# Fourth layer's dense attention: one head at a time instead of two by turns

## The chip, the cores and the metric

The kernel runs on one core of one Trainium2 chip. The metric is the device time of one execution in microseconds; a kernel's time is the median of its runs. Beside the times there is one profiled execution of the kernel, taken by the hardware profiler. All stretches below are microseconds from the start of that execution's span.

## What is computed

The program chains convolution-like and attention layers on a batch of 4 with 128 channels and 32x32 positions, that is 4 x 1024 tokens of 128 features. The change touches one of them, `_L3_attn_ref`, whose dense part is this:

```python
def global_mha(x, in_w, in_b, out_w, out_b, nh):      # B, S, D = 4, 1024, 128; nh = 8
    hd = D // nh                                       # 16
    q, k, v = qkv_proj(x, in_w, in_b)                  # each [B, S, nh, hd]
    scores = jnp.einsum('bqhd,bkhd->bhqk', q, k) / np.sqrt(hd)
    attn = jax.nn.softmax(scores, axis=-1)
    o = jnp.einsum('bhqk,bkhd->bqhd', attn, v).reshape(B, S, D)
    return o @ out_w.T + out_b
# beside it a local attention (window 5, 4 heads) on the same x; both are fused by a
# two-layer MLP with silu, added to x and normalised; a second MLP with silu follows
```

4 batches of 8 heads make 32 heads; each has a 1024 x 1024 matrix of scores. All of this is in float32; the kernel carries q and k as three bfloat16 parts stacked on 96 rows.

## The kernel before

The change lies in `fourth_layer_stream`, which writes out the order of every engine's work for the whole fourth layer. A **step** is one tile of 128 keys (`m`, 0 to 7) of one head: 256 steps in all, 64 in each batch. For a step TensorE multiplies two halves of 512 queries into the three banks of `f_ST` (`scores_transposed`, line 2179), ScalarE takes the exponential of each half into `f_probs` (line 2369), which holds four steps, and TensorE then multiplies `f_v_ext` (values of the head, 16 columns and a column of ones, padded to 32) by these probabilities and adds them up over the eight tiles in the bank `f_O` (`mix`, line 2196). `mix` is called for two steps at a time (`VISIT` = 2), on every odd step from the third on: a *visit*, of four float32 products, each of which is two records of the trace, so eight records. Where in `f_O` a product lands is set by

```python
h, m = steps[s]
for n in range(NC2):
    at = 32 * (NC2 * (h % SHARE) + n)
    last = nc.tensor.matmul(O[at:at + 32, :], f.v_ext[...], f.probs[...], start=(m == 0),
                            stop=(m == NT - 1), tile_position=(0, at))
```

so head parity and query half choose one of the four strips of 32 columns of the array and 32 partitions of the bank. In the order before, steps go through two heads of a group (`SHARE` = 2) by turns: tile 0 of the even head, tile 0 of the odd head, tile 1 of the even head, and so on; 16 steps (`IN_GROUP`) make a group.

The exponential needs a shift for each query, the maximum of its row. Therefore TensorE also computes the scores the other way round, queries on partitions (`scores`, line 2152), two halves for each tile of 128 queries, into the two banks of `f_ring`, and VectorE reduces each half (`maximum`, line 2486). After a head's last half VectorE splits the shifts into three bfloat16 parts (`parts`, lines 2495 to 2499), TensorE turns them into rows (`shift_rows`, line 2164, in the same `f_ring`), and ScalarE copies these to three more rows of `f_stacks` (`rows`, line 2346, two copies). `scores_transposed` of tile 0 of a head waits for that copy (`rows_off`). The list `items`, made by `schedule` and `schedule_rows`, sets which halves of maxima and which rows go with which step; `AHEAD` = 2 is the number of tiles by which the maxima run ahead of a whole group of 16 tiles. Before the first step, with no other stream work beside it, the list "first" holds the maxima and rows of two heads.

Beside the steps run the programs `pre` (normalisation, q, k, v of the next batch), `local` (local attention) and `tail` (output projection, MLPs, normalisations of the batch before). `Beside.turn` lets them go on after each half of a step; their due times are counted in halves of steps. After the last step, `tally` follows and the next layer begins. SP loads `f_stacks` for a group eight steps after the group four before it ended (`LOAD_AFTER`), and ScalarE carries `f_O` off two steps after each group (`carry_off`).

The first layer has an attention of the same make (`dense_attention`), with heads of 32 features: there the values are padded to 64 columns, one head is taken at a time, and a visit (line 702, `att_O`) is four products too, at columns 0, 64, 0, 64.

Of the kernel before, what the change touches and what calls it, by code (L numbers as in the profile page):

```python
# [14 lines left out]
B, IMG = 4, 32  # L15
N = IMG * IMG
NT = N // P
# [1775 lines left out]
class Fourth:  # L1793


    HD, HEADS, SHARE, GROUPS = 16, 8, 2, 4
    IN_GROUP = SHARE * NT
# [64 lines left out]
def fourth_layer(nc, k):  # L1862

    with ExitStack() as c:
        f = Fourth(nc, k, c)
        with ExitStack() as c2:
            fourth_layer_stream(nc, k, f, c2)
        clear(nc, f.semaphores)
        nc.all_engine_barrier(sem_only=True)


def fourth_layer_stream(nc, k, f, c):

    HD, HEADS, SHARE, GROUPS, IN_GROUP = f.HD, f.HEADS, f.SHARE, f.GROUPS, f.IN_GROUP
    STEPS, VISIT, PROBS, RING, HALVES, TURNS = f.STEPS, f.VISIT, f.PROBS, f.RING, f.HALVES, f.TURNS
    steps = [(b * HEADS + g * SHARE + j, m) for b in range(B) for g in range(GROUPS) for m in range(NT)
             for j in range(SHARE)]
    all_groups = B * GROUPS
    lag = VISIT + 1

# [2 lines left out]
    def schedule(step, lo, hi):  # L1883
        new = [("s", h, t, n) for h, t in (divmod(r, NT) for r in range(lo, min(hi, B * HEADS * NT)))
               for n in range(NC2)]
        at_step[step] = list(range(len(items), len(items) + len(new)))
        items.extend(new)

    def schedule_rows(step, h):
        rows_at[step] = rows_at.get(step, []) + [h]  # L1890
        item_of_rows[h] = len(items)
        items.append(("r", h))

    schedule("first", 0, IN_GROUP)
    for h in range(SHARE):
        schedule_rows("first", h)
    for s in range(len(steps)):
        r = s + IN_GROUP + f.AHEAD
        schedule(s, IN_GROUP if s == 0 else r, r + 1)
        if (s + 1) % NT == 0 and s + IN_GROUP < len(steps):  # L1900
            schedule_rows(s, (s + IN_GROUP) // NT)
    order, count = {}, {"s": 0, "r": 0}
    for i, item in enumerate(items):
        order[i] = count[item[0]]
# [1768 lines left out]
```

## Time and profile before

| | us |
|---|---|
| median of the runs | 2507.49 |
| the profiled execution, its own time | 2505.68 |
| its span, first to last instruction | 2503.9 |
| fourth layer, the two heads of maxima ahead of the first step | 1334 to 1361 |
| fourth layer, the 256 steps | 1362 to 2080 |
| tally, then the next layer | 2080 to 2504 |

The profile names instructions by line and tile: `f_O<-f_probs,f_v_ext 128*32 128x512` is a product with a 128x32 stationary and a 128x512 moving operand. Busy time is the union of an engine's records; a matmul's record includes its way through the array, so consecutive matmuls overlap, and the distance from one start to the next is what one costs in a stream. PEclk is the granted clock of TensorE, where 1.00 is 2.4 GHz and 0.50 is 1.2 GHz.

### The profile page before, as it was taken

What the parts mean: (1) busy time and instruction counts of PE and PEld (TensorE: products, weight loads), DVE (VectorE), ACT (ScalarE), POOL (GpSimd) and SP (SyncE); (2) the same over time, 40 slices, a digit from 0 to 9 for tenths busy, and PEclk for the clock granted to TensorE, in tenths of its full rate; (3) what the DMA queues carried; (4) which work ended last, traced back from release to release, by engine and by line L of the source; (5) the groups of instructions that cost most, each with busy time, mean ns of one, the idle gap of its engine ahead of it and who ended that gap; (6) DMA issues with size and microseconds to landing.
All of it is one profiled execution on the core that took longest, in us unless ns stands there. A gap on an engine that the chain in (4) does not pass through costs nothing. (4 is left out here: it accounts for less than half of the span.)

```text
span 2503.9 us, 26613 instructions
## 1 busy us (share of the span) xinstructions
PE 1892.9 (76%) x8906; PEld 869.7 (35%) x8906; DVE 1573.4 (63%) x3594; ACT 1021.7 (41%) x1662; POOL 714.1 (29%) x693
## 2 busy tenths in 40 slices
PE   1595786689578657579975888878878888978596
PEld 1121321332132124456641222322322325854356
DVE  3477778777776866645745575665566555634567
ACT  0241233314123314535542667656656662124251
POOL 2300630260063023014442312322322331137720
PEclk7696887789688878879975999989988987769797
DMA  3300300210030000021002111101011000024100
GB/s 100 92 3 25 83 9 20 60 40 2 25 92 1 20 8 1 1 81 39 1 17 75 41 30 38 32 27 39 28 28 37 4 4 14 2 62 52 10 4 35
DMA packets 55407, 80.26 MB, mean 32 GB/s; under 512 B 17201, under 2 KB 28455, under 8 KB 55024
## 3 DMA queue, kind: packets, MB, share of 16 engines
q1 hardware_dynamic: 44758, 69.14, 9.3%
q10 hardware_dynamic: 6426, 7.99, 1.4%
q0 software_dynamic: 4096, 1.58, 1.3%
q8 instruction: 62, 1.02, 0.2%
q14 instruction: 65, 0.53, 0.1%
HBM read 50.13 MB, written 24.68 MB: 30 GB/s over the span
## 5 line engine op out<-in xcount | busy, mean ns | idle before, releaser
L2486 DVE TENSOR_REDUCE f_half_max<-f_ring 128x1 f32<-128x512 f32 x512 | 334.8, 684 | 273.0 <-PE f_ring L2152 270.9
L2369 ACT ACTIVATE f_probs<-f_ST 128x512 f32<-128x512 f32 x512 | 292.8, 597 | 210.8 <-PE f_ST L2179 206.7
L2152 PE MATMUL f_ring<-f_stacks 96*128 96x512 bf16 x512 | 212.1, 415 | 54.5 <-DVE f_half_max L2486 28.1
L772 DVE TENSOR_REDUCE att_half_max<-att_ring 128x1 f32<-128x512 f32 x256 | 161.2, 683 | 101.5 <-PE att_ring L659 96.6
L2179 PE MATMUL f_ST<-f_stacks 99*128 99x512 bf16 x512 | 204.0, 403 | 10.4 <-ACT f_probs L2369 10.3
L755 ACT ACTIVATE att_probs<-att_ST 128x1024 f32<-128x1024 f32 x128 | 129.3, 1023 | 156.1 <-PE att_ST L684 155.9
L2196 PE MATMUL f_O<-f_probs,f_v_ext 128*32 128x512 f32 x1024 | 153.3, 674 | 0.1
L3202 POOL DMA_INDIRECT ti_row<-features,slot_from x128 | 126.9, 992 | 57.4 <-issue 57.4
L2152 PEld LDWEIGHTS f_ring<-f_stacks 96*128 96x128 bf16 x512 | 50.4, 99 | 258.8 <-DVE f_half_max L2486 162.6
L659 PE MATMUL att_ring<-stacks 96*128 96x512 bf16 x256 | 103.7, 471 | 46.5 <-DMA stacks<-parts_dram 25.9
L684 PE MATMUL att_ST<-stacks 96*128 96x512 bf16 (+1 forms) x512 | 137.8, 398 | 0.0
L702 PE MATMUL att_O<-att_probs,v_ext 128*64 128x512 f32 x512 | 132.7, 644 | 6.6 <-DVE att_den L791 6.6
L1242 DVE TENSOR_TENSOR loc_weighed<-loc_wide,l_pad 128x512 f32<-128x512 f32 x200 | 124.4, 683 | 14.6 <-PE loc_wide L1196 9.5
L1739 ACT ACTIVATE bm_h<-bm_ps,bn 128x512 f32<-128x512 f32 x128 | 99.5, 777 | 78.2 <-PE bm_ps L1706 72.9
L1762 POOL TENSOR_TENSOR bm_h<-bm_h,bm_mix 128x512 f32<-128x512 f32 x64 | 81.9, 1302 | 159.7 <-ACT bm_h L1739 159.7
L1053 POOL MEMSET loc_padded<- 104x1296 f32 x4 | 4.7, 1177 | 387.5 <-POOLq L43 387.5
L1224 POOL TENSOR_TENSOR loc_partial<-loc_partial,loc_weighed 128x512 f32<-128x512 f32 x88 | 110.0, 1271 | 10.1 <-DVE loc_weighed L1242 6.6
L1202 PE MATMUL loc_acc<-loc_weighed,turned 128*128 128x512 f32 x208 | 107.1, 599 | 0.4
L2757 PE MATMUL gm_ps<-xn_cm,x 128*128 128x512 f32 x128 | 66.0, 644 | 45.8 <-ACT turned L2805 35.4
L2060 PE MATMUL f_ring<-f_hot 128*64 128x64 bf16 x1024 | 90.5, 366 | 7.9 <-DVE f_hot L2504 7.9
L2060 PEld LDWEIGHTS f_ring<-f_hot 128*64 128x64 bf16 x1024 | 87.1, 272 | 22.4 <-issue 12.7
L2504 DVE TENSOR_SCALAR f_hot<-f_xn 128x256 bf16<-128x256 bf16 x512 | 72.3, 220 | 28.7 <-issue 14.7
(585 smaller groups left out, 3552.7 us busy)
## 6 DMA issues: line engine op xcount, KB each, us to landing
f_stacks<-f_parts SPq DMA_DIRECT2D x192, 64.0 KB, 2.2
parts_dram<-l_parts SPq DMA_DIRECT2D x8, 768.0 KB, 3.6
stacks<-parts_dram SPq DMA_DIRECT2D x24, 256.0 KB, 9.5
stacks<-parts_dram ACTq DMA_DIRECT2D x24, 256.0 KB, 10.5
f_parts<-f_parts SPq DMA_DIRECT2D x8, 768.0 KB, 3.4
es_raw<-L_ffn_edge_index SPq DMA_DIRECT2D x8, 512.0 KB, 4.2
bm_mix<-mix SPq DMA_DIRECT2D x8, 512.0 KB, 9.0
xn_cm<-x SPq DMA_DIRECT2D x1, 2048.0 KB
```

The lines of the kernel that those rows point to most:

```text
L684: last = nc.tensor.matmul(ST[:, s % 2, n * BANK:(n + 1) * BANK], k.stacks[0:rows, 1, per * h + j, m * P:(m + 1) * P], k.stacks[0:rows, 0, ...
L702: last = nc.tensor.matmul(O[at:at + width, :], k.v_ext[:, m, h, :], probs[:, s % probs_ring, n * BANK:(n + 1) * BANK], start=(m == 0), sto ...
L755: nc.scalar.activation(probs[:, s % probs_ring, :], ST[:, s % 2, :], ACT.Exp).then_inc(probs_ready, 1)
L772: nc.vector.tensor_reduce(half_max[:, h % 2, t, n:n + 1], ring[:, i % RING], AX.X, ALU.max, negate=True).then_inc(reduced, 1)
L1242: nc.vector.tensor_tensor(o_, a, v, ALU.mult).then_inc(weighed_ready, 1)
L2060: last = nc.tensor.matmul(bank[64 * a:64 * a + 64, 0:64], low, high, start=(start and m == ms[0]), stop=(stop and m == ms[-1]), tile_posit ...
L2152: nc.tensor.matmul(ring[:, i % RING], f.stacks[0:STACK, 0, at, t * P:(t + 1) * P], f.stacks[0:STACK, 1, at, n * BANK:(n + 1) * BANK], star ...
L2179: nc.tensor.matmul(ST[:, i % HALVES], f.stacks[0:STACK + 3, 1, h % HEADS, m * P:(m + 1) * P], f.stacks[0:STACK + 3, 0, h % HEADS, n * BANK ...
L2196: last = nc.tensor.matmul(O[at:at + 32, :], f.v_ext[:, h // HEADS % 2, m, h % HEADS, :], f.probs[:, s % PROBS, n * BANK:(n + 1) * BANK], s ...
L2369: nc.scalar.activation(f.probs[:, s % PROBS, n * BANK:(n + 1) * BANK], ST[:, i % HALVES], ACT.Exp).then_inc(probs_ready, 1)
L2486: nc.vector.tensor_reduce(f.half_max[:, h % 2, t, n:n + 1], ring[:, i % RING], AX.X, ALU.max, negate=True).then_inc(reduced, 1)
L3202: self.nc.gpsimd.indirect_dma_start(self.row[:, j, :], None, self.k.features, bass.IndirectOffsetOnAxis(ap=self.k.slot_from[:, j:j + 1], a ...
```

## The change

The steps go through the heads one after the other, all eight tiles of a head, then the next head. The maxima run ahead by one head and two tiles (8 + 2) instead of two heads and two tiles (16 + 2), and "first" holds one head. The rows of head h come with the step just before its first, 8h - 1; before, they came nine steps ahead of an even head and two ahead of an odd one. Sizes of buffers, `VISIT`, `AHEAD`, the groups, their loads and the programs beside the steps stay.

```diff
-    steps = [(b * HEADS + g * SHARE + j, m) for b in range(B) for g in range(GROUPS) for m in range(NT)
-             for j in range(SHARE)]
+    steps = [(h, m) for h in range(B * HEADS) for m in range(NT)]
@@
-    schedule("first", 0, IN_GROUP)
-    for h in range(SHARE):
-        schedule_rows("first", h)
+    schedule("first", 0, NT)
+    schedule_rows("first", 0)
     for s in range(len(steps)):
-        r = s + IN_GROUP + f.AHEAD
-        schedule(s, IN_GROUP if s == 0 else r, r + 1)
-        if (s + 1) % NT == 0 and s + IN_GROUP < len(steps):
-            schedule_rows(s, (s + IN_GROUP) // NT)
+        r = s + NT + f.AHEAD
+        schedule(s, NT if s == 0 else r, r + 1)
+        if (s + 1) % NT == 0 and s + NT < len(steps):
+            schedule_rows(s, (s + NT) // NT)
```

## Rows read from the trace of the kernel before

**Rows 1.** The page's first part: busy time, share of the span, instructions.

```profile
PE 1892.9 (76%) x8906; PEld 869.7 (35%) x8906; DVE 1573.4 (63%) x3594; ACT 1021.7 (41%) x1662; POOL 714.1 (29%) x693
```

**Rows 2.** Busy time by stretch: stretch, length, engines, PEclk, DMA share, GB/s.

```profile
1334.00:1362.00 28.00, 22.00 (x52) 4.29 (x52) 23.43 (x44) 2.31 (x4) 2.54 (x3) 0.50 0.29 82
...
1362.00:2080.00 718.00, 601.93 (x2969) 191.57 (x2968) 430.20 (x1013) 454.09 (x849) 197.29 (x243) 0.93 0.09 27
2030.00:2080.00 50.00, 40.11 (x182) 10.38 (x180) 18.56 (x84) 30.86 (x63) 24.73 (x38) 0.80 0.03 6
```

**Rows 3.** Lines, 1362 to 2080: busy us, mean ns | idle before, releaser.

```profile
L2486 DVE TENSOR_REDUCE f_half_max<-f_ring 128x1 f32<-128x512 f32 x479 | 313.5, 684 | 251.1 <-PE f_ring L2152 250.4
L2369 ACT ACTIVATE f_probs<-f_ST 128x512 f32<-128x512 f32 x512 | 292.8, 597 | 210.8 <-PE f_ST L2179 206.7
L2179 PE MATMUL f_ST<-f_stacks 99*128 99x512 bf16 x512 | 204.0, 403 | 10.4 <-ACT f_probs L2369 10.3
L2152 PE MATMUL f_ring<-f_stacks 96*128 96x512 bf16 x477 | 191.3, 401 | 31.2 <-DVE f_half_max L2486 24.3
L2196 PE MATMUL f_O<-f_probs,f_v_ext 128*32 128x512 f32 x1024 | 153.3, 674 | 0.1
```

**Rows 4.** TensorE's timeline between two visits: start, length, instruction, [idle before, releaser].

```profile
1450.22 1.06 PE L2196 MATMUL f_O<-f_probs,f_v_ext 128*32 128x512 f32 x8
1451.21 0.39 PE L2152 MATMUL f_ring<-f_stacks 96*128 96x512 bf16 x1
...
1452.39 0.39 PE L2152 MATMUL f_ring<-f_stacks 96*128 96x512 bf16 x1
1452.62 0.38 PE L2179 MATMUL f_ST<-f_stacks 99*128 99x512 bf16 x1
1453.70 0.39 PE L2152 MATMUL f_ring<-f_stacks 96*128 96x512 bf16 x1 [0.70 <-DVE f_half_max L2486]
...
1454.24 1.07 PE L2196 MATMUL f_O<-f_probs,f_v_ext 128*32 128x512 f32 x8
```

**Rows 5.** First layer's attention: the page's group of its visits, and TensorE's timeline.

```profile
L702 PE MATMUL att_O<-att_probs,v_ext 128*64 128x512 f32 x512 | 132.7, 644 | 6.6 <-DVE att_den L791 6.6
...
173.52 1.94 PE L702 MATMUL att_O<-att_probs,v_ext 128*64 128x512 f32 x8
175.39 1.92 PE L684 MATMUL att_ST<-stacks 96*128 96x512 bf16 x8
```

**Rows 6.** TensorE's timeline around a fall of its clock.

```profile
1480.53 0.60 PE L2164 MATMUL f_ring<-ident_b,f_shift_parts 128*3 128x128 bf16 x8 [0.90 <-DVE f_half_max L2486]
...
1481.60 1.94 PE L2196 MATMUL f_O<-f_probs,f_v_ext 128*32 128x512 f32 x8
1483.47 0.58 PE L2047 MATMUL f_side<-f_att_t,spread 60*128 60x512 bf16 x1
```

**Rows 7.** TensorE's timeline ahead of the first step.

```profile
1334.24 1.03 PE L2152 MATMUL f_ring<-f_stacks 96*128 96x512 bf16 x2 [18.76 <-DMA f_stacks<-f_parts]
...
1357.46 0.60 PE L2164 MATMUL f_ring<-ident_b,f_shift_parts 128*3 128x128 bf16 x8 [0.28 <-DVE f_half_max L2486]
1359.01 0.60 PE L2164 MATMUL f_ring<-ident_b,f_shift_parts 128*3 128x128 bf16 x8 [0.94 <-DVE f_shift_parts L2499]
```

**Rows 8.** Rows of a head: TensorE, ScalarE, and who waited for the copies.

```profile
1444.15 0.40 PE L2164 MATMUL f_ring<-ident_b,f_shift_parts 128*3 128x128 bf16 x8 [0.30 <-DVE f_half_max L2486]
...
1444.80 1.07 PE L2196 MATMUL f_O<-f_probs,f_v_ext 128*32 128x512 f32 x8
...
1446.02 0.38 PE L2179 MATMUL f_ST<-f_stacks 99*128 99x512 bf16 x1
...
1444.60 1.16 ACT L2346 CAST f_stacks<-f_ring 3x512 bf16<-3x512 f32 x2 [0.50 <-PE f_ring L2164]
...
  PE f_ring L2152: 0.7, 1
```

## The prediction

> **What bounds the kernel now.** I read the page first: TensorE is the busiest engine over the whole span, 76% [rows 1]. An average over many layers settles nothing here, so the next view is the busy time by stretch, cut to the part that the change reorders. The 256 steps take 718 us, 2.80 us a step or 5.61 us a pair of steps. In them TensorE is busy 601.9 us (84%), ScalarE 454.1, VectorE 430.2 [rows 2]. The lines of that stretch say who waits for whom: VectorE idles 250 us for scores that TensorE has not made yet, ScalarE 207 us for its transposed scores, while TensorE's own waits ahead of these two lines are 31 and 10 us [rows 3]. So TensorE sets the pace, with 718 - 602 = 116 us of idle time in small pieces. A timeline of one pair shows one kind of piece: after a visit of 0.99 us, TensorE makes two halves of scores, then finds both banks of the ring full; the third half comes 1.18 us after the first, and the fourth waits 0.70 us more for a maximum [rows 4]. These waits hang on scores that were issued *after* the visit. That matters below: a longer visit doesn't shorten them.
>
> **The visits (the large term).** No instruction is added or removed; what moves is which four products stand in one visit. Before, a visit holds tile m of the even head and tile m of the odd head: strips 0, 32, 64, 96, four different ones. After, it holds tiles m and m+1 of one head: strips 0, 32, 0, 32 (or 64, 96, 64, 96). The third product adds to the strip of the first and needs the same columns of the array. Before, eight records whose mean is 674 ns, 5.4 us if laid end to end, take 153.3/128 = 1.20 us of TensorE per visit: four strips work at a time [rows 3]. The trace has the other case too. In the first layer a visit is four products of the same 128x512 moving size on columns 0, 64, 0, 64, two strips at a time. Its 512 records are 64 visits in 132.7 us, 2.07 us each; at full clock one takes 175.39 - 173.52 = 1.87 us from its start to the next instruction, against 0.99 us in the fourth layer [rows 4, 5]. The only difference is width, 64 columns for 32, and the moving operand of 512 columns is what takes time in both. So the added time is 2.07 - 1.20 = 0.87 us a visit, the same 0.88 at full clock, and 128 x 0.87 = +112 us of TensorE time. From below, if every visit ran at full clock, it is 128 x 0.87 = 111, the same. From above: where the clock is at 0.50, a visit before takes 1.87 us [rows 6], so two rounds would take about 3.74, +1.87. The mean clock of the stretch, 0.93 [rows 2], means 14% of the time at half clock; with 18 of 128 visits there it is 110 x 0.87 + 18 x 1.87 = +129. I take 112.
>
> By the Trainium skill, TensorEngine Tiling (Array Packing), section Theoretical Speedup, tiles of up to 32 columns give up to fourfold speed and tiles of up to 64 up to twofold; an estimate by that factor doubles the 1.20 us, +153 us and a sum of 2626. The trace's own ratio is smaller, 2.07/1.20 = 1.73.
>
> **How much of it is hidden.** A longer visit gives VectorE and ScalarE time to catch up, so a TensorE wait that hangs on something older than the visit shrinks. Of 116 us idle the waits as in rows 4 stay, since their chain (score, maximum, next score) begins behind the visit. What can shrink is a backlog: a side job of VectorE or ScalarE that began before the visit. The bounds are 0 and half, about 60: the 24 us for maxima and the 10 us for probabilities [rows 3] are a minority of the idle time, and the rest is in many small waits of the programs beside, whose due times are counted in steps and so get later too. VectorE and ScalarE are idle 40% and 37% of the stretch, so a backlog is rare. I take a quarter nearer to the lower end, 27 us.
>
> **Maxima ahead of the first step.** The 32 halves take 1357.46 - 1334.24 = 23.2 us, 0.73 each, with VectorE busy 23.4 of 28 us, and the second head's rows another 1.55 [rows 2, 7]. After, 16 halves and one head's rows: -11.6 - 1.6 = -13.2 us. The 16 halves are not gone. Before, the last 18 steps (2030 to 2080) have no maxima; after, only the last ten. Eight steps thus gain 16 halves, at 0.22 us each (the distance in a stream, 1452.62 - 1452.39 [rows 4]) to 0.68 (a reduction [rows 3]): +3.6 to +11. Those last steps took 2.78 us each without maxima, no less than the others, at a clock of 0.80 [rows 2], so something else set their pace and the halves may be cheap; I take +7. Net -6, between -10 and -2. It is also all that the change can win by itself.
>
> **The shorter lead at a head's start.** Rows of head h now come at step 8h - 1, and the first transposed scores of head h follow directly, so TensorE waits there on ScalarE's two copies, with whatever ScalarE does before them. The positions inside eight steps are the same as before (last maxima two steps earlier, rows at the eighth step, on odd steps with a visit behind them), only the head that they serve is nearer. In one such place before, the rows start at 1444.15, the copies run from 1444.60 to 1445.76, and TensorE, after a transposed half and a visit, reaches the next transposed half at 1446.02 [rows 8]. The cover holds by 0.26 us, and a visit longer by 0.87 us makes it 1.1. Besides, TensorE already waited for the same copies before, one matmul later: the ring has two banks, so the second half of scores behind the rows needs the rows' bank. In the whole trace that wait is 0.7 us, once [rows 8]. Price 0; at most 0.22 us at 31 heads, +7, if one matmul of cover were just missing. With no cover at all, each head costs the copies and their start, 1445.76 - 1444.48 = about 1.3 us, +40.
>
> **What stays.** SP's loads of stacks come at the same steps, while the maxima of a group now begin eight steps later: more room. The carrying off of `f_O`, the ring of four probabilities and the programs beside keep their steps. ScalarE and VectorE do the same instructions. These cost nothing, hidden by the 264 and 288 us that the two engines idle [rows 2].
>
> **The sum.** 2505.7 (own time of the profiled execution) + 112 - 27 - 6 + 0 = 2584.7, say **2585 us**, +3.2%. The median of the runs is 2507.5, 1.8 above the profiled one, which is nothing beside the other terms.
>
> **The rivals.**
> *Not slower: the idle time swallows the visit.* TensorE has 116 us idle; if each added 0.87 us took its place, the time would be 2505.7 + 112 - 112 - 6 = 2500. It decides (within 2%, below 2557) from 112 - 6 - 51 = 55 us hidden on, half of the idle time. For it: 84% busy is not 100%. Against: the waits begin behind the visit [rows 4], and VectorE and ScalarE mostly wait for TensorE [rows 3]. 12%.
> *The clock gives it back.* After waits such as 0.90 us TensorE's work runs at half clock, a visit 1.87 us instead of 0.99 [rows 4, 6]. With longer visits TensorE idles less, and the 14% at half clock (100 us) could go: full speed would do that work in 50. With half of that, 25 us, won, the time is 2560; with all, 2535. The reverse is possible as well. The Trainium skill, TensorE: Matmul & The Clock Gate, section What's actually happening, has the low clock as the default that activity lifts; these rows agree with its direction, and they show no effect of the number of strips. 12%, half of it within 2%.
> *Each head's start stalls.* TensorE drains and waits for ScalarE's copies 31 times: +40, 2625. Against it stands the cover of rows 8. 6%.
> *Strips don't matter.* If the third and fourth product overlapped the first two, only -6 is left: 2500. Against it stand the first layer's visits [rows 5]. 3%.
>
> **How the numbers follow.** My forecast has 67%, with a range of its own from 2557 to 2640: the lower end has half of the idle pieces hidden, the upper 2505.7 + 129 - 2 + 7 = 2640 with nothing hidden. Rivals 12 + 12 + 6 + 3. About 2% is what a measurement of this kernel can tell from no change. Slower by over 2%: 67 + 6 + 6 = 79, and one more from a partly swallowed case, 80%. Within 2%: 19%. Faster: 1%, since no term wins more than 13 us. The range from 2545 to 2640 leaves out the fully swallowed and overlapping cases and most of the clock's best case, about 15 in 100, and the rest above.
>
> **What would show it.** Right: `f_O`'s busy time grows from 153 to about 265 us at the same 1024 records and about the same mean; a visit takes 1.87 us at full clock; the 256 steps take 718 + 112 - 27 + 7 = 810 us and TensorE's busy share rises above 87%; the waits of VectorE and ScalarE for TensorE grow by tens of us each; the stretch ahead of the first step shrinks by 13 us. Wrong: visits that stay near 1 us, a step time that stays at 2.8 us with TensorE's idle time gone, a granted clock well away from 0.93, or waits of `f_ST` for `f_stacks` of 1 us and more at each eighth step.

## The result and the profile after

| | before | changed |
|---|---|---|
| median, us | 2507.49 | 2567.11 |
| ratio, 95% interval | | 1.0235 [1.0215, 1.0255] |
| profiled execution, us | 2505.68 | 2569.27 |
| first maxima to first step, us | 1334.2 to 1361.7: 27.5 | 1333.9 to 1349.3: 15.5 |
| the 256 steps, us | 1361 to 2080: 719 | 1349 to 2143: 794 |
| after the steps, us | 423 | 424 |

The median before leaves out one of four runs, a slow one of 2756.47 us. The change makes the kernel some 59 us slower. All of it lies in the steps: 75 us more there, 12 less ahead of them, 1 more behind. (The two profiled executions lie 63.6 us apart, a few us more than the medians; the accounts in us below are of profiled executions.) Line numbers of the changed kernel are two lower from here on. Busy time by stretch (stretch, length, PE, PEld, DVE, ACT, POOL, PEclk, DMA share, GB/s), first the steps of the kernel before, counted from 1361, then the changed kernel, against [rows 2]:

```profile
1361.00:2080.00 719.00, 602.93 (x2971) 191.76 (x2970) 430.68 (x1013) 454.09 (x849) 197.29 (x243) 0.93 0.09 27
...
1334.00:1349.00 15.00, 10.97 (x27) 2.10 (x26) 11.88 (x22) 1.16 (x2) 2.54 (x3) 0.50 0.50 141
1349.00:2143.00 794.00, 692.83 (x2995) 216.63 (x2993) 444.38 (x1042) 457.10 (x851) 196.95 (x243) 0.96 0.09 25
```

TensorE's busy share of the steps rises from 84% to 87%, and its clock from 0.93 to 0.96. The lines of that stretch in the changed kernel, against [rows 3]:

```profile
L2484 DVE TENSOR_REDUCE f_half_max<-f_ring 128x1 f32<-128x512 f32 x495 | 324.0, 684 | 324.8 <-PE f_ring L2150 324.4
L2367 ACT ACTIVATE f_probs<-f_ST 128x512 f32<-128x512 f32 x512 | 293.4, 596 | 268.6 <-PE f_ST L2177 264.4
L2194 PE MATMUL f_O<-f_probs,f_v_ext 128*32 128x512 f32 x1024 | 259.8, 631 | 0.0
L2177 PE MATMUL f_ST<-f_stacks 99*128 99x512 bf16 x512 | 198.8, 391 | 9.6 <-ACT f_probs L2367 8.0 <-ACT f_stacks L2344 1.5
L2150 PE MATMUL f_ring<-f_stacks 96*128 96x512 bf16 x495 | 194.9, 394 | 29.7 <-DVE f_half_max L2484 21.0 <-ACT f_stacks L2344 0.7
```

The same 1024 records of `f_O`, no longer one by one (631 ns on average against 674), take 259.8 us instead of 153.3: two work at a time where four did. VectorE and ScalarE wait 74 and 58 us longer for TensorE. The same place of TensorE's timeline as [rows 4], changed kernel:

```profile
1450.94 1.91 PE L2194 MATMUL f_O<-f_probs,f_v_ext 128*32 128x512 f32 x8
1452.78 0.39 PE L2150 MATMUL f_ring<-f_stacks 96*128 96x512 bf16 x1
...
1453.96 0.39 PE L2150 MATMUL f_ring<-f_stacks 96*128 96x512 bf16 x1
1454.18 0.38 PE L2177 MATMUL f_ST<-f_stacks 99*128 99x512 bf16 x1
1455.65 0.39 PE L2150 MATMUL f_ring<-f_stacks 96*128 96x512 bf16 x1 [1.09 <-DVE f_half_max L2484]
...
1456.19 1.91 PE L2194 MATMUL f_O<-f_probs,f_v_ext 128*32 128x512 f32 x8
```

The visit takes 1.84 us to the next instruction, against 0.99. Behind it the pattern is the same: the third half of scores still comes 1.18 us after the first, and the fourth still waits for a maximum, 1.09 us here. Ahead of the first step one head is left, as against [rows 7]:

```profile
1333.85 1.04 PE L2150 MATMUL f_ring<-f_stacks 96*128 96x512 bf16 x2 [18.79 <-DMA f_stacks<-f_parts]
...
1346.63 0.60 PE L2162 MATMUL f_ring<-ident_b,f_shift_parts 128*3 128x128 bf16 x8 [1.82 <-DVE f_shift_parts L2497]
...
1349.34 0.63 PE L2177 MATMUL f_ST<-f_stacks 99*128 99x512 bf16 x1
```

### The profile page after: what moved, and what is told of

The parts are those of the page before. It is cut to its first block and busy times, and to the rows that moved or that the text cites. A ratio compares the mean times of both kernels' runs of the same rounds, so it can differ in the third digit from the quotient of the medians.

```text
span 2567.5 us, 26614 instructions
## 1 busy us (share of the span) xinstructions
PE 1972.4 (77%) x8906; PEld 891.7 (35%) x8906; DVE 1572.0 (61%) x3594; ACT 1023.6 (40%) x1662; POOL 713.3 (28%) x693
## 5 line engine op out<-in xcount | busy, mean ns | idle before, releaser
L2194 PE MATMUL f_O<-f_probs,f_v_ext 128*32 128x512 f32 x1024 | 259.8, 631 | 0.0
L2150 PE MATMUL f_ring<-f_stacks 96*128 96x512 bf16 x512 | 205.0, 401 | 50.0 <-DVE f_half_max L2484 22.5
L2177 PE MATMUL f_ST<-f_stacks 99*128 99x512 bf16 x512 | 198.8, 391 | 9.6 <-ACT f_probs L2367 8.0
L755 ACT ACTIVATE att_probs<-att_ST 128x1024 f32<-128x1024 f32 x128 | 129.4, 1024 | 156.7 <-PE att_ST L684 156.5
L2194 PEld LDWEIGHTS f_O<-f_probs,f_v_ext 128*32 128x32 f32 x1024 | 50.3, 113 | 137.4 <-issue 122.8
```

The costliest lines, as they stand in the source:

```text
L755: nc.scalar.activation(probs[:, s % probs_ring, :], ST[:, s % 2, :], ACT.Exp).then_inc(probs_ready, 1)
L2150: nc.tensor.matmul(ring[:, i % RING], f.stacks[0:STACK, 0, at, t * P:(t + 1) * P], f.stacks[0:STACK, 1, at, n * BANK:(n + 1) * BANK], star ...
L2177: nc.tensor.matmul(ST[:, i % HALVES], f.stacks[0:STACK + 3, 1, h % HEADS, m * P:(m + 1) * P], f.stacks[0:STACK + 3, 0, h % HEADS, n * BANK ...
L2194: last = nc.tensor.matmul(O[at:at + 32, :], f.v_ext[:, h // HEADS % 2, m, h % HEADS, :], f.probs[:, s % PROBS, n * BANK:(n + 1) * BANK], s ...
```

## The experiments

The theory: the price is the strips, and neither the order of the heads nor the short lead costs anything. The rivals: the order or the lead is the price; and, for the part of the added work that doesn't show in the time, a share of each microsecond is hidden, or a fixed stock is used up first.

### Strips against order: two runs with one edit

The same line was edited in both kernels. In the changed kernel it puts the four products of a visit back on four strips; in the kernel before it puts them on two.

```diff
-                    at = 32 * (NC2 * (h % SHARE) + n)
+                    at = 32 * (NC2 * (m % 2) + n)
```

(The flags that open and close a sum go with it. In both runs values are added up in strips where they don't belong, so the dense attention isn't computed; the instructions stay.)

> The changed kernel (one head at a time), but the strip of a product is chosen by the parity of its tile instead of its head, so the two tiles of a visit stand on four different strips again. The even and odd tiles of a head are then summed apart and the second head of a group overwrites the first, so the sums of the dense attention aren't the reference's; every instruction stays. Theory (strips set the price): a visit falls from 1.84 to 1.0 us at full clock, f_O's busy time from 260 to about 155 us, the steps from 793 to about 720 us, and the 12 us saved ahead of the first step stay: 2490 to 2505 us. Rival (the order of heads or the short lead costs the time): it stays above 2540 us.

Measured: 2503.8 us beside 2506.45 of the kernel before on the same chip, ratio 0.9986 [0.9973, 1.0000]. Lines and steps of this run:

```profile
L2194 PE MATMUL f_O<-f_probs,f_v_ext 128*32 128x512 f32 x1024 | 153.0, 673 | 0.1
L2177 PE MATMUL f_ST<-f_stacks 99*128 99x512 bf16 x512 | 203.2, 400 | 11.2 <-ACT f_probs L2367 10.5 <-ACT f_stacks L2344 0.7
L2150 PE MATMUL f_ring<-f_stacks 96*128 96x512 bf16 x495 | 200.4, 405 | 33.9 <-DVE f_half_max L2484 26.5 <-ACT f_stacks L2344 0.7
1351.00:2081.00 730.00, 609.76 (x2995) 194.98 (x2993) 440.67 (x1031) 455.32 (x851) 197.26 (x243) 0.93 0.10 27
```

> The kernel before (two heads by turns, long lead), with the same single edit: the strip is chosen by the parity of the tile, so both heads of a visit stand on the same two strips. Both heads are summed into one another, so the dense attention's sums aren't the reference's; every instruction stays. Theory (strips): a visit rises from 1.0 to 1.84 us, f_O's busy time from 153 to about 260 us and the steps from 718 to about 790 us, without the gain ahead of the first step: 2575 to 2590 us. Rival (order or lead): it stays at 2508 us, within 10 us.

Measured: 2575.9 us, ratio 1.0276 [1.0256, 1.0297].

```profile
L2196 PE MATMUL f_O<-f_probs,f_v_ext 128*32 128x512 f32 x1024 | 262.6, 638 | 0.0
1364.00:2152.00 788.00, 693.29 (x2971) 217.57 (x2969) 434.61 (x1019) 455.51 (x849) 196.90 (x243) 0.95 0.09 25
```

The time goes with the strips and not with the order. With four strips the order of the change is as fast as the kernel before, 0.3% faster at most; with two strips the order before is as slow as the change, and a little slower still (1.0276 against 1.0235). A strip is 32 columns of the array and 32 partitions of the bank, chosen by one number, so these runs don't tell which of the two the third product waits for. The first run also tells what the shorter start is worth by itself: 12 us less ahead of the steps, 730 - 719 = 11 more in them, where the 16 halves of maxima now run beside steps (7 of the 11 are work of TensorE, 609.76 - 602.93, and 4 idle time). By the medians about 3 us are left of it.

### The lead

The edit against the changed kernel, cut: where the maxima and rows are scheduled, `NT` becomes `IN_GROUP` again.

```diff
-    schedule("first", 0, NT)
-    schedule_rows("first", 0)
+    schedule("first", 0, IN_GROUP)
+    for h in range(SHARE):
+        schedule_rows("first", h)
@@
-        r = s + NT + f.AHEAD
+        r = s + IN_GROUP + f.AHEAD
...
```

> One head at a time as in the changed kernel, but the maxima and rows keep the lead of the kernel before (two heads and two tiles, both heads ahead of the first step). Theory: the short lead costs nothing at the heads' starts and saves 12 us ahead of the first step, of which about 3 come back later: 2573 to 2580 us, 6 to 12 above the changed kernel. Rival (each head's start stalls for the rows): the long lead wins more than it costs, below 2560 us, and TensorE's waits for f_stacks, 2.2 us in the changed kernel, go to 0.

Measured: 2572.89 us, ratio 1.0254 [1.0235, 1.0272]. That is 0.2%, 5 us, above the changed kernel's 1.0235, on the side that the theory expected and a little less than its 6 to 12, but the two intervals overlap. The second run of the lead, against the changed kernel:

```diff
-    AHEAD = 2
+    AHEAD = 4
@@
-        if (s + 1) % NT == 0 and s + NT < len(steps):
+        if (s + 3) % NT == 0 and s + NT < len(steps):
```

> The changed kernel with a lead of four tiles instead of two and a head's rows two steps earlier, at step 8h - 3, so that ScalarE's copies have two steps more of cover. Theory: there is nothing to win but the 2.2 us that TensorE waits for f_stacks, against two tiles more ahead of the second step: within 4 us of the changed kernel, 2563 to 2571. Rival (stalls at the heads' starts, whatever shows as idle): a gain of 10 us or more, below 2557.

Measured: 2570.76 us, ratio 1.0254 [1.0237, 1.0271], by the ratio 5 us above the changed kernel, with overlapping intervals. Who waited for ScalarE's copies of the rows, and what TensorE waited for, over the whole trace, first in the changed kernel, then in this run:

```profile
  PE f_ST L2177: 1.5, 3
  PE f_ring L2150: 0.7, 1
...
L2150 PE MATMUL f_ring<-f_stacks 96*128 96x512 bf16 x512 | 205.0, 401 | 50.0 <-DVE f_half_max L2484 22.5
```

```profile
L2150 PE MATMUL f_ring<-f_stacks 96*128 96x512 bf16 x512 | 207.8, 407 | 59.4 <-DVE f_half_max L2484 31.9 <-DMA f_stacks<-f_parts 18.8 <-ACT f_stacks L2344 0.7
L2177 PE MATMUL f_ST<-f_stacks 99*128 99x512 bf16 x512 | 200.0, 394 | 8.2 <-ACT f_probs L2367 8.1
```

The 1.5 us of `f_ST` are gone, and the time isn't lower; TensorE waits longer for maxima, 31.9 us against 22.5. Neither a longer lead nor more cover for the rows wins anything, so the short lead isn't the cause.

### How much of the added work shows

Two runs of the kernel before with other doses: every second visit on two strips, and all four products of a visit on one strip. (The flags of the sums go with the strips again.)

```diff
-                    at = 32 * (NC2 * (h % SHARE) + n)
+                    pair = h % SHARE if v % 2 == 0 else v // 2 % 2
+                    at = 32 * (NC2 * pair + n)
```

> The kernel before, with every second visit on two strips and the others on four; the sums of the dense attention aren't the reference's, every instruction stays. It asks how the time grows with the added TensorE work, of which all 128 visits add 106 us and bring 70 to 75. Theory A (a share of each added us is hidden, about 30%): half the visits bring half the time, +35, about 2541. Theory B (a fixed stock of some 31 us of idle time is used up first): 53 - 31 = +22, about 2529.

Measured: 2546.6 us, ratio 1.0145 [1.0123, 1.0168], which is +36, near theory A's +35.

```profile
L2197 PE MATMUL f_O<-f_probs,f_v_ext 128*32 128x512 f32 x1024 | 203.0, 640 | 0.1
1364.00:2125.00 761.00, 650.61 (x2971) 205.66 (x2971) 433.49 (x1018) 454.51 (x849) 197.46 (x243) 0.94 0.09 26
```

```diff
-                    at = 32 * (NC2 * (h % SHARE) + n)
+                    at = 32 * (v % 4)
```

> The kernel before, with all four products of a visit on one strip (the strip changes from visit to visit), so they run one after the other; the sums of the dense attention aren't the reference's, every instruction stays. A visit is four rounds, about 3.5 us at full clock, +2.5 for each of 128: 325 us of added TensorE work. Theory A (30% of each added us is hidden): +225, about 2732. Theory B (a fixed stock of 31 us is used up first, the rest counts in full): +294, about 2800. If strips were not the price, 2508.

Measured: 2758.65 us, ratio 1.0991 [1.0968, 1.1015], which is +249, between the two expectations.

```profile
L2196 PE MATMUL f_O<-f_probs,f_v_ext 128*32 128x512 f32 x1024 | 477.6, 612 | 0.0
1361.00:2339.00 978.00, 905.61 (x2971) 272.50 (x2971) 434.58 (x1039) 455.76 (x849) 197.04 (x243) 0.97 0.07 20
```

From the profiled executions, TensorE's account of the steps in us; "other work" is its busy time less `f_O`, idle is length less busy:

| order by turns | steps | f_O | other work | idle | clock |
|---|---|---|---|---|---|
| before, four strips | 719 | 153 | 450 | 116 | 0.93 |
| every second visit on two | 761 | 203 | 448 | 110 | 0.94 |
| two strips | 788 | 263 | 431 | 95 | 0.95 |
| one strip | 978 | 478 | 428 | 72 | 0.97 |

By these executions 8 of 50 added us are hidden, 40 of 109 and 65 of 324; by the ratios of the runs 14, 40 and 75. (The execution profiled for the first dose was the longest of its four, 2549.14 us.) Both theories fall: 30% of 324 would be 97, and a stock of 31 us would hide 31 at every dose. The half dose by itself would have agreed with theory A.

Three things hide the added work. The idle time melts slowly, by 6, 21 and 44 us. The other work falls by 2, 19 and 22 us, and the records of the traces show two parts of this. Products of the local attention (`f_side`, line 2023) run beside the longer visits, on strips that these leave free: 1, 5 and 9 us more of other work lie inside visits than in the kernel before. The rest, 1, 14 and 12 us, are shorter records, as the clock is higher. From two strips to one the other work gives little more, and 215 us of work bring 190 of time.

### A version between the two

The shorter start without the price: only the first group goes head by head. The edit against the changed kernel, cut:

```diff
+    steps = [(h, m) for h in range(SHARE) for m in range(NT)]
+    steps += [(b * HEADS + g * SHARE + j, m) ...][IN_GROUP:]
@@
+    done, early = NT, {7: 1, 11: 2, 15: 3}
     for s in range(len(steps)):
+        upto = s + NT + f.AHEAD + 1 + min(NT * (s + 1) // IN_GROUP, NT)
+        schedule(s, done, upto)
...
```

> The kernel before, but the first group alone goes head by head: only one head's maxima and rows stand ahead of the first step, and the lead grows to that of the kernel before in the first 16 steps; from the second group on everything is as before. Theory: -12 us ahead of the first step, +0.84 us for each of 8 visits on two strips (+7, of which 2 hidden), and 16 halves of maxima made beside the steps (+3): 2500 to 2508, 1 to 8 below the kernel before. Rival: in the first steps VectorE, with three halves a step, becomes the bound and gives it all back: 2508 to 2515.

Measured: 2516.83 us, ratio 1.0038 [1.0022, 1.0054], so slower than the kernel before by 9 us: the rival's way, and a little beyond its 2515. Its steps take 744 us. All of them, the first of them by stretch, and its `f_O`:

```profile
1348.00:2092.00 744.00, 624.62 (x2995) 197.56 (x2992) 441.64 (x1032) 456.54 (x851) 197.28 (x243) 0.92 0.09 26
1348.00:1360.00 12.00, 10.57 (x23) 1.68 (x20) 11.40 (x35) 4.18 (x7) 2.00 (x10) 0.50 0.05 14
1360.00:1395.00 35.00, 29.88 (x111) 8.66 (x112) 18.37 (x42) 19.06 (x36) 2.86 (x5) 0.86 0.00 1
...
L2201 PE MATMUL f_O<-f_probs,f_v_ext 128*32 128x512 f32 x1024 | 162.0, 676 | 0.1
```

VectorE is busy 11.4 of the first 12 us, with TensorE at half clock; the visits of this run take 8.7 us more than before. Of the 25 us more in the steps another 13 are TensorE's other work (624.62 - 162.0 against 602.93 - 153.3) and 3 idle time; why the other work grew by 13, where the same 16 halves cost 7 in the first experiment, isn't settled. No version of these beats the kernel before clearly.

### The order within a visit

The changed kernel, with the loops over steps and halves exchanged: strips 0, 0, 32, 32.

```diff
-            for s in range(v * VISIT, (v + 1) * VISIT):
-                h, m = steps[s]
-                for n in range(NC2):
+            for n in range(NC2):
+                for s in range(v * VISIT, (v + 1) * VISIT):
+                    h, m = steps[s]
```

> The changed kernel with the four products of a visit in another order: strips 0, 0, 32, 32 instead of 0, 32, 0, 32. The result and every instruction stay. If TensorE starts products strictly in the order in which they stand, the second waits for the first, the third runs beside the second and the fourth waits for the third: three rounds, 2.7 us a visit at full clock against 1.84, f_O's busy time about 370 us, 2635 to 2650 us. If it starts a later product on a free strip past one that waits (the one-strip run shows products of another line starting among a visit's last records), two rounds are left: f_O's busy time about 260 us and 2562 to 2572 us, as in the changed kernel.

Measured: 2576.98 us, ratio 1.0259 [1.0235, 1.0284], against 1.0235 of the changed kernel, with overlapping intervals; 2577 is 5 us above the upper end of what two rounds were expected to give. A line and a visit of this run:

```profile
L2194 PE MATMUL f_O<-f_probs,f_v_ext 128*32 128x512 f32 x1024 | 265.5, 642 | 0.0
...
1451.58 1.92 PE L2194 MATMUL f_O<-f_probs,f_v_ext 128*32 128x512 f32 x8
1453.43 0.39 PE L2150 MATMUL f_ring<-f_stacks 96*128 96x512 bf16 x1
```

The visit takes 1.85 us: two rounds, not three. On two strips it is their number that counts, and not which of these two orders the four products are written in.

## Why the prediction came out as it did

**What bounds.** Right: TensorE sets the pace of the steps. 106.5 us more on it brought 75 us more time, while VectorE and ScalarE did the same work and waited longer.

**The visits.** Right in kind, a little high: +112 predicted, +106.5 measured. At full clock a visit came to 1.84 us, not the first layer's 1.87. The Trainium skill, TensorEngine Tiling (Array Packing), section Theoretical Speedup, has up to fourfold speed for 32 columns and up to twofold for 64; the estimate by that factor doubled the visit. The trace has 259.8/153.3 = 1.69 over the steps and 1.84/0.99 = 1.86 at full clock, so the row was the better source than the page's "up to".

**What is hidden.** This term was mis-sized, and mostly by its place. I looked for it in TensorE's waits alone and took 27 us, which was a choice between 0 and 60 and not worked out from a row. With 106.5 us of longer visits and the 11 us that the 16 halves brought to the steps (first experiment), the steps should have grown by 117.5; they grew by 75. So 42 are hidden. That run, with the change's order and four strips, is what to compare with. Idle time gave 19 us (120 there, 101 after), less than I took, and the reason that I gave for this held in the main: the waits behind a visit stay, as the timeline after shows, though those for maxima fell from 26.5 us there to 21.0. The other 24 came out of TensorE's other work, busy time less `f_O`: 457 there, 433 after. Its products are the same, and two things made them cheaper.

The first is that some now run beside a visit. The products of the local attention, line 2021, stand on strips 0 and 32 behind some visits. Before, they started when the visit was nearly over; now the visits of an odd head leave strips 0 and 32 free, and 8 of the 20 groups start with the visit. The kernel before, then the changed one:

```profile
1431.54 1.06 PE L2196 MATMUL f_O<-f_probs,f_v_ext 128*32 128x512 f32 x8
1432.42 1.03 PE L2023 MATMUL f_side<-f_prod,place 128*20 128x512 f32 x4
...
1430.71 0.62 PE L2194 MATMUL f_O<-f_probs,f_v_ext 128*32 128x512 f32 x2
1430.73 0.61 PE L2021 MATMUL f_side<-f_prod,place 128*20 128x512 f32 x2
1431.16 0.60 PE L2194 MATMUL f_O<-f_probs,f_v_ext 128*32 128x512 f32 x2
1431.18 0.60 PE L2021 MATMUL f_side<-f_prod,place 128*20 128x512 f32 x2
1431.59 1.03 PE L2194 MATMUL f_O<-f_probs,f_v_ext 128*32 128x512 f32 x4
```

That is 8 of the 24 us: other work that lies inside visits grew from 18 to 26 us. The second, 16 us, is shorter records: `f_ST` has 391 ns on average, 400 in that run and 403 before, at the same median of 381 in all three, so fewer of its records ran at half clock.

**The clock rival.** It was one of the rivals with 12%, and a part of it happened beside my forecast. The clock of the steps rose from 0.93 to 0.96; time at half clock went from 14% of 719, 101 us, to 8% of 794, 64 us. 37 us less at half clock are worth some 18 us of work, near those 16. The Trainium skill, TensorE: Matmul & The Clock Gate, section What's actually happening, says that activity lifts the clock; the doses agree, 0.93, 0.94, 0.95, 0.97. This is an order of few runs: those with every visit on two strips lie between 0.94 and 0.96 themselves, and none sets the clock by itself. My fault was to treat it as an alternative to the forecast; a longer stay on a busy engine should have carried this as a term of its own sum.

**The start.** -13.2 predicted, -12.0 measured. That the 16 halves come back was right, but +7 was predicted and 11 measured, the upper end of what I gave, so the net is -1, not -6; the whole kernel with four strips, at ratio 0.9986, puts it at about -3.

**The shorter lead.** Right: priced at 0. TensorE waits 2.2 us in all for the rows, and taking 1.5 of these away won nothing.

**The sum.** 2505.7 + 106.5 - 42 - 12 + 11 = 2569.2, and the profiled execution has 2569.3; this closes because the 42 is itself the difference. (The steps took 794 us, not the 810 that I had named.) Against my 2585 the visits account for -5.5, the hidden part for -15, the start for +5. So the mechanism was right, and the number came near although the hidden part came in good part from places that the forecast didn't have. The rivals of a swallowed visit, of stalls at the heads' starts and of strips that don't matter fell: the first needed 55 us hidden, of which 42 came, the second showed 2.2 us, the third the opposite.

## What to carry to other kernels

A reordering that adds and removes no instruction can still change what runs at the same time: look at which strips of the array neighbouring small products use before changing the order of loops. A price taken from another stage of the same trace with the same number of strips came within some 5%. When an engine that is not full gets more work, ask not only which of its waits shrink, but also whether its other work gets cheaper or finds room beside the new.

## What the runs showed of the hardware

In these runs TensorE starts products out of their written order when a strip is free. With strips 0, 0, 32, 32 written next to each other a visit still took 1.85 us. In the changed kernel, products on strips 0 and 32 that are written behind a visit start 0.02 us after it (1430.73 against 1430.71, above). In the one-strip run, `f_side` products (strips 0 and 32), which are written behind the whole visit, start among its last records. TensorE's timeline of the one-strip run:

```profile
1457.70 2.33 PE L2196 MATMUL f_O<-f_probs,f_v_ext 128*32 128x512 f32 x5
1459.44 0.61 PE L2023 MATMUL f_side<-f_prod,place 128*20 128x512 f32 x2
1459.87 0.59 PE L2196 MATMUL f_O<-f_probs,f_v_ext 128*32 128x512 f32 x1
1459.88 0.60 PE L2023 MATMUL f_side<-f_prod,place 128*20 128x512 f32 x2
1460.30 1.02 PE L2196 MATMUL f_O<-f_probs,f_v_ext 128*32 128x512 f32 x2
```

The two lines change off at 1459.44, 1459.87, 1459.88 and 1460.30. Four strips are also not quite four times as fast as one: the same four products took 0.99 us on four strips, 1.84 on two, and, at full clock in the one-strip run, 3.56 on one (its visit at 1451.83 is followed by the next instruction at 1455.39).
